# A gated graph network on one core: gates that wait bank by bank, and a step of the symmetric counts moved ahead

## The reference, cut to what matters

```python
for l in range(4):
    m = x @ weight[l]
    agg = segment_sum(m[src], dst, num_segments=n_nodes)
    gi = agg @ w_ih.T + b_ih
    gh = x @ w_hh.T + b_hh
    r = sigmoid(i_r + h_r); z = sigmoid(i_z + h_z)
    n = tanh(i_n + r * h_n)
    x = (1.0 - z) * n + z * x
return x + node_embed
```

## Time and profile before

| | us |
|---|---|
| median of 3 runs | 3267.45 (3265.71 to 3273.17) |
| the profiled execution | 3268.28 |
| span of its trace | 3265.8 |
| TensorE busy | 2968.8 (91%) |
| VectorE busy | 2186.7 (67%) |
| ACT busy | 897.4 (27%) |

### The profile page before, as it was taken

One profiled execution on the slowest core, in us unless ns is written; L12 is line 12 of the kernel. 1 busy time (PEld: TensorE's weight loads), 2 busy tenths in 40 slices (PEclk: granted clock), 3 DMA queues, 4 the chain that ended last, 5 costly groups with the idle time before them and its releaser, 6 DMA issues. The chain is left out here.

```text
span 3265.8 us, 47549 instructions
## 1 busy us (share of the span) xinstructions
PE 2968.8 (91%) x18761; PEld 1780.3 (55%) x18761; DVE 2186.7 (67%) x4024; ACT 897.4 (27%) x1685; POOL 16.7 (1%) x23
## 2 busy tenths in 40 slices
PE   2888779999897999999979999989999998999997
PEld 2566445555343554545545665655656564656665
DVE  7999445555326777776657666686667586666676
ACT  3888422111111000000023222233222233222222
POOL 2000000000000000000000000000000000000000
PEclk8999989999998999999989999999999999999999
DMA  5455247676004655554330000020000002000001
GB/s 125 147 149 160 82 143 224 219 225 196 22 1 138 175 153 167 166 160 126 100 114 3 4 3 4 3 81 4 3 7 4 3 17 69 3 4 3 4 3 41
DMA packets 310958, 265.84 MB, mean 81 GB/s; under 512 B 32767, under 2 KB 289409, under 8 KB 308174
## 3 DMA queue, kind: packets, MB, share of 16 engines
q1 hardware_dynamic: 296558, 259.28, 25.9%
q10 hardware_dynamic: 13760, 2.61, 0.4%
q0 software_dynamic: 416, 0.85, 0.1%
HBM read 172.67 MB, written 90.05 MB: 80 GB/s over the span
## 5 line engine op out<-in xcount | busy, mean ns | idle before, releaser
L1708 PE MATMUL psum<-r_wd,r_h 128*128 128x512 fp8e4 (+1 forms) x2600 | 568.0, 375 | 13.7 <-ACT r_h L229 13.4
L2283 PE MATMUL psum<-m_agg,m_weights 128*128 128x512 f16 (+2 forms) x2016 | 422.0, 362 | 33.3 <-ACT m_agg L2190 33.3
L2244 PE MATMUL psum<-counts,m_h 128*128 128x512 fp8e4 (+2 forms) x2100 | 417.5, 355 | 12.6 <-DVE m_h L1987 12.6
L2302 PE MATMUL psum<-m_weights,x_nodes 128*128 128x256 f16 (+1 forms) x3600 | 413.0, 273 | 17.0 <-DVE m_wtmp L2097 15.4
L1708 PEld LDWEIGHTS psum<-r_wd,r_h 128*128 128x128 f16 x2600 | 241.5, 97 | 307.5 <-issue 15.5
L2302 PEld LDWEIGHTS psum<-m_weights,x_nodes 128*128 128x128 f16 (+1 forms) x3600 | 350.1, 98 | 74.7 <-DVE m_wtmp L2097 22.1
L2283 PEld LDWEIGHTS psum<-m_agg,m_weights 128*128 128x128 f16 x2016 | 196.8, 101 | 241.2 <-issue 49.3
L2244 PEld LDWEIGHTS psum<-counts,m_h 128*128 128x128 f16 x2100 | 206.3, 98 | 210.3 <-issue 21.3
L2202 ACT ACTIVATE m_hT<-m_hT,m_g 128x256 f32<-128x256 f32 x300 | 135.4, 500 | 599.1 <-DVE m_hT L2111 599.1
L2190 ACT ACTIVATE m_agg<-psum,x_nodes 128x512 f32<-128x512 f32 (+2 forms) x336 | 236.3, 716 | 143.7 <-PE psum L2283 113.7
L2111 DVE SCALAR_TENSOR_TENSOR m_hT<-psum,x_nodes,m_bias 128x512 f32<-128x512 f32 (+1 forms) x150 | 112.0, 750 | 169.8 <-PE psum L2319 169.7
(11 more groups left out here) (298 smaller groups left out, 3275.6 us busy)
## 6 DMA issues: line engine op xcount, KB each, us to landing
r_wd<-packed_sym SPq DMA_DIRECT2D x120, 640.0 KB, 4.1
packed_counts<-strip SPq DMA_DIRECT2D x21, 1800.0 KB, 7.8
sym_blocks<-packed_counts SPq DMA_DIRECT2D x88, 384.0 KB, 4.6
packed_sym<-sym_blocks SPq DMA_DIRECT2D x84, 384.0 KB, 3.3
w_stage<-in_L_gnn_strong_W SPq DMA_DIRECT2D x12, 1024.0 KB, 6.7
m_weights<-in_L_gnn_strong_W SPq DMA_DIRECT2D x21, 512.0 KB, 4.7
x_parked<-x_nodes SPq DMA_DIRECT2D x2, 1600.0 KB, 5.9
x_nodes<-x_parked SPq DMA_DIRECT2D x2, 1600.0 KB, 6.3
```

What stands on the lines that cost most here:

```text
L1708: m = pe.matmul(bank[pair[b]][:, 0:2 * cw], h16[:, part, p0 + i, :], f_[:, 2 * b:2 * b + 2, :], start=(p0 + i == 0 and part == 0), stop=(p ...
L2244: m = pe.matmul(bank[kb][:, 0:cw], h16[:, part, i, kb * P:(kb + 1) * P], A[:, i, c_:c_ + cw], start=(i == 0 and part == 0), stop=(i == NT ...
L2283: m = pe.matmul(bank[4 + hh % 2][:, 0:cw], w_[:, i, kb, f * P:(f + 1) * P], agg16[:, j, kb, 0:cw], start=(x_ == 0), stop=(x_ == len(todo) ...
L2302: m = pe.matmul(bank[b_][0:r_, 0:H], s_[:, pa[0] * BANK + k * P:pa[0] * BANK + k * P + r_], w_[:, pa[1], f, :], start=(f == 0 and pa == PA ...
```

## The change

It has four edits. TensorE's gate_b waits for each bank by itself: BR for g_reset_kept, BZ for g_update_kept, BH for g_gated (which the first operation of the gated sum sets), and gate_c waits for g_gated_sum ahead of BI. One more step of the symmetric counts stands ahead of layer 0's loop, on TensorE and on VectorE, so that all later steps use the other bank than before, and the last chunk has one step less. VectorE's gate_c is cut into `gated` and `state`. In layer 0's loop from chunk 1 on, `state` stands behind finish and the step; in layers 1 to 3 it stands behind the step of tile 13 ("Sd"), where before it followed the gated sum at tile 11.

```diff
-        AMONG = {1: "S", 3: "a", 4: "S", 6: "S", 7: "b", 9: "S", 11: "c", 13: "S", 16: "S", 19: "S", 22: "S"}
+        AMONG = {1: "S", 3: "a", 4: "S", 6: "S", 7: "b", 9: "S", 11: "c", 13: "Sd", 16: "S", 19: "S", 22: "S"}
...
-                    if n:
-                        pe.wait_ge(g_reset_kept, n)
-                        pe.wait_ge(g_update_kept, n)
-                        pe.wait_ge(g_gated_sum, n)
-                    for g, bk in enumerate((BR, BZ, BH)):
+                    for g, (bk, left) in enumerate(((BR, g_reset_kept), (BZ, g_update_kept), (BH, g_gated))):
+                        if n:
+                            pe.wait_ge(left, n)
...
                     for g, (bk, made_of) in enumerate(((BR, g_reset), (BZ, g_update), (BI, g_input))):
+                        if bk == BI and n:
+                            pe.wait_ge(g_gated_sum, n)
...
                 sum_chunk(0, EARLY + 1, gates_of=0)
+
+                sym.pe_step(other)
                 for ci in range(1, NCH):
...
-                gate_c(0, ci)
+                gated(0, ci)
                 if ci == 0:
+                    state(0, ci)
                     gate_a(0, EARLY + 1)
-                if ci:
+                    sym.dve_step()
+                else:
                     finish(0, ci - 1)
                     sym.dve_step()
+                    state(0, ci)
...
                             if what == "c" and gates_of is not None:
-                                gate_c(l, gates_of)
+                                gated(l, gates_of)
+
+                            if what == "d" and gates_of is not None:
+                                state(l, gates_of)
...
                             gate_a(l, ci)
-                            gate_c(l, ci)
+                            gated(l, ci)
+                            state(l, ci)
```

More of the change, by code:

```diff
@@ L1138, in state_low, with gated @@
                                              ALU.subtract).then_inc(made, 1)
[L1140 to L1143, removed]
+                def gated(l, ci):
+                    n, q, cw = l * NCH + ci, ci % 2, CH[ci][1]
+                    r_, t_ = rr[q][:, 0:cw], tt[q][:, 0:cw]
                     vec.wait_ge(g_reset_kept, n + 1)
@@ L1149, in gate_c, with state @@
                     vec.tensor_tensor(t_, t_, bank[BI][:, 0:cw], ALU.add).then_inc(g_gated_sum, 1)
+                def state(l, ci):
+                    n, q = l * NCH + ci, ci % 2
+                    c_, cw = CH[ci]
+                    h_, z_, t_, n_ = ht[:, c_:c_ + cw], zz[q][:, 0:cw], tt[q][:, 0:cw], nn[q][:, 0:cw]
                     vec.wait_ge(g_new, n + 1)
```

## The result

| | before | after |
|---|---|---|
| median, us | 3267.19 (4 runs, 3265.71 to 3273.17) | 3244.69 (4 runs, 3242.79 to 3246.46) |
| profiled execution, us | 3268.28 | 3242.79 |
| span of its trace, us | 3265.8 | 3240.4 |

The ratio, worked out from all the runs, is 0.9928, with a 95% interval of 0.9913 to 0.9944: faster, by 0.7% (the two medians alone give 0.9931). The forecast was 3243.8.

The account below looks back on a forecast made before the run. Layer 0's step sharing bank 7 with the turn, and the lowered clock behind it, bound the kernel. -24.3 - 9.8 + 10.4 = -23.7 us, from 3267.45 to 3243.8; range 3236 to 3256.

Parts of the forecast that it names:

- What bounds the kernel: Layer 0: the step sharing bank 7 with the turn waits for the low half, about 4 us, then the clock falls.
- Part 1: Layer 0's loop: an extra step ahead moves the step behind the turn to bank 6, state made later; -24.3 us.
- Its two terms: Layer 0: 22.8 us gained over the five periods of gated sums, another 1.6 behind the last gated sum.
- The lower bound of part 1: Layer 0: -29 us if TensorE's and ACT's waits overlap better, the round not below VectorE's busy time.
- the 6.9 us: Layer 0: VectorE's busy time per period, taken as the least a round could take.
- Part 2: Layers 1 to 3: state behind the step of tile 13 removes waits at tile 19; -9.8 us, bounds -13 to -6.
- Part 3: Layers 1 to 3: changed bank parity makes steps behind turns wait for the low half; +10.4 us, bounds +6 to +16.
- The rivals: Clock stays low in layer 0: 3256, 0.10; stalls drop clock: 3275, 0.03; wait only moves: 3262-3267, 0.05; better case 3235, 0.08.
- The wait for a piece at step 12: Layer 0: piece 6 loads late in SP's queue; costed at nothing, or a few us once without cover.

Follow-up runs that it names:

- e2_step_ahead: Kernel before with only one more step on TensorE and VectorE ahead of layer 0's loop: 3258.38 us, ratio 0.9962.
- e5: Changed kernel with gate_b's three waits in one place again and no wait of gate_c's own for the gated sum: 3244.02 us, ratio to before 0.9923.
- e7: e4's kernel with ACT making layer 0's state_high and high half of the chunk before ahead of the Tanh: 3225.94 us, ratio to before 0.9864.
- e1: Kernel before with only the state moved behind the step of tile 13 in layers 1 to 3: 3253.40 us, ratio 0.9948.
- e3: Changed kernel with the state right behind the gated sum again in layers 1 to 3: 3257.01 us, ratio to before 0.9959.
- e4: Changed kernel with one more step on each engine behind layer 0's last sum tiles, restoring bank parity in layers 1 to 3: 3235.51 us, ratio to before 0.9893.
- e6: Changed kernel with VectorE's state ahead of finish in layer 0, as before: 3248.04 us, ratio to before 0.9934.
- e8: Changed kernel with the edits of e5 and e6 together, state first and old waits: 3246.18 us, ratio to before 0.9926.
- e9: e6's kernel run once more, unchanged, on the same chip as e8: 3247.48 us, ratio to before 0.9932.

## Why the prediction was right, point by point

**What bounds the kernel** held: the step on bank 7 behind the turn, and the clock behind it, were the price of layer 0's chunks. e2_step_ahead took 23.0 us off layer 0 with the bank alone.

**Part 1** was forecast at -24.3 and measured -24.2. The five periods were 8.2, 7.6, 8.0, 7.6 and 7.4 after a forecast of 8.3, 7.6, 8.1, 7.7 and 7.4; the tail was 8.42 (419.89 to 428.31) after 8.0. (Its two terms, 22.8 and 1.6, add up to 24.4.) Following VectorE's list in its new order, row by row, with the handover to it at 0.1 us, was enough. What the waits by bank carry was not priced by itself; e5 shows that with the state later it is nothing. The lower bound of part 1 rested on the 6.9 us that e7 shows to be too high; it was not reached here.

**Part 2** had the right mechanism and the wrong size: -9.8 forecast, -13.3 measured alone (e1) and 13.2 the other way (e3). The failed term is the count of what there was to win. I took the idle times of the list (13.8 us in thirteen waits), and these leave out some 0.15 us of each stall: from start to start they are 15.9 us. That is 2.1 of the 3.5 us. Most of the rest is in what I left standing. At tile 22 of the six 384-column chunks I put 0.2 to 0.3 each (the figures beside it, 485.13 and 485.26, give 0.13); in e1 it was 0.24 and 0.26 in two of them and under 0.1 in the others. The wait left in the 309-column chunks (0.77) came as 0.59 in the changed kernel's list, 0.75 from start to start. Taken together, the steps' stalls in layers 1 to 3, without those for the low half, were 17.4 us from start to start before and 4.2 in e1 (short ones included that the list does not show): 13.1 of the 13.3 measured.

**Part 3** was +10.4 forecast and +10.3 measured (e2), 10.4 the other way (e4). In e2 some 1.3 of it were waits for loads, so that agreement is in part luck; e4 has none. Here I had worked from start to start and not from the list: the eight stalls of layers 1 and 2 were put at 1.3 each and came as 1.07 to 1.48, 10.5 together, and the four of layer 3, put at 0.6, as 0.47 to 0.78.

**The sum.** -24.2 - 13.3 + 10.3 = -27.2, and the network as a whole gave -27.4. The median moved by 22.5 and the profiled execution by 25.5; what lies between is the part ahead of layer 0 (here +1.4), the rest behind the network (+0.7) and the runs' own spread. So that 3243.8 came within 1 us of 3244.69 is in part luck: part 2 was short by 3.5 us, and these took it back.

**The rivals.** The clock stayed at 1.00 over layer 0's loop, with the exception of its last wait (2.33 us, then 2.96 for eight matmuls), and at 0.98 in layers 1 to 3 in spite of twelve new stalls. The Trainium skill ("TensorE: Matmul & The Clock Gate", section on psum-queue depth-cycling) says that TensorE's clock goes to and fro where the engine idles briefly between groups often enough. With the changed kernel's waits of 0.6 to 1.4 us this trace does not show it. In e6, e8 and e9 half speed followed single waits of 1.96 to 2.63 us at two chunks; whether that is what the section means, these runs do not show. The wait for a piece at step 12 did not come: TensorE shows no wait for a load in the changed kernel.

## What to carry to other kernels

When two users share PSUM banks in turn, count the parity through every loop that follows: one step more at the front took 23 us off layer 0 and cost 10 us in the layers behind it, and one step more behind the first loop gave them back. Price a wait by the starts of the instructions around it and not by the idle time beside it, which was shorter by some 0.15 us each time here and zero for a stall of 0.24 us. After a wait is gone, look at which engine's list now comes last and whether its order fits: here moving ACT's copies ahead of the Tanh was worth 6.8 us in one stage, where the release of the banks for single waits was worth nothing.

## What the runs showed of the hardware that I had not expected

Half clock followed a wait of 1.96 us, did not follow one of 1.95 or one of 2.96, and stood at the same two chunks in three profiles (e6, e8, e9). With the same waits of 3.8 to 4.5 us, the five periods of layer 0 took 62.3 us in the profile before and 59.8 in that of e1, and what differs is the clock behind the waits. So this stage moved by 2.5 us without any change to it; with waits near 2 us (e2 against e8) it moved by 3.4.
